# A decoder block: the order of SyncE's transfers within a quarter of the cross-attention loop, and the memory layout of its bias rows

## What is computed

```
# self-attention: one head, causal; only the row sums of exp(scores) are used
o = exp_qk.sum(-1);  y = relu(o @ fc1_w.T + fc1_b) @ fc2_w.T + fc2_b
x = layernorm(x + y)
# cross-attention: 16 heads of 32, keys = values = ctx, queries = x
logits  = einsum('bhqd,bhkd->bhqk', q, k) + bias
weights = softmax(logits / sqrt(32))
x = layernorm(x + (weights @ v) @ w_out)
# feed-forward with quantised weights (127 steps) and activations (32767 steps)
x = layernorm(x + q16(gelu(q16(x) @ q8(W_in) + b_in)) @ q8(W_out) + b_out)
```

## Time and profile before

| | before |
|---|---|
| three runs, us | 2289.72, 2265.87, 2286.9 |
| median, us | 2286.9 |
| profiled execution, us | 2284.26 |
| its span, us | 2282.5 |
| PE busy | 2111.4 us (93%) |
| DVE busy | 1735.8 us (76%) |
| ACT busy | 1082.4 us (47%) |
| POOL busy | 822.0 us (36%) |
| queue of SP's transfers, share of 16 DMA engines | 46.0% |
| queue of POOL's transfers, share | 22.9% |

### The profile page before, as it was taken

How to read it: one execution, slowest core, us unless ns; L and a number is a source line. 1 busy time by engine, 2 the same in 40 slices (tenths; PEclk the granted TensorE clock), 3 DMA queues, 4 the chain that set the end, 5 groups by cost and what they waited for, 6 DMA issues and landing times.

```text
span 2282.5 us, 32943 instructions
## 1 busy us (share of the span) xinstructions
PE 2111.4 (93%) x11904; PEld 1167.9 (51%) x11904; DVE 1735.8 (76%) x3296; ACT 1082.4 (47%) x1522; POOL 822.0 (36%) x802
## 2 busy tenths in 40 slices
PE   7999999984798998999999859999999699999997
PEld 3444444431586776777777524444444344444443
DVE  6768686865677897898898656777666488888885
ACT  1444444443444555555555224444444565555551
POOL 2122221222125555556455432222222134444442
PEclk9999999996779999999999779999999899999999
DMA  6334243457749969979975437888888656666662
GB/s 233 108 126 155 94 148 110 115 137 176 188 128 208 260 166 191 279 183 208 262 181 153 136 84 267 288 288 289 267 270 272 249 195 227 224 233 230 226 226 79
DMA packets 386626, 448.46 MB, mean 196 GB/s; under 512 B 279270, under 2 KB 279430, under 8 KB 368032
## 3 DMA queue, kind: packets, MB, share of 16 engines
q1 hardware_dynamic: 322448, 286.07, 46.0%
q0 software_dynamic: 64016, 160.28, 22.9%
HBM read 258.93 MB, written 138.73 MB: 174 GB/s over the span
## 4 chain that ended last, share of the span: by engine, by line
PE 82%; DVE 7%; issue 6%; ACT 1%; DMA 1%; POOL 1%; SPq 0%; DVEq 0%; POOLq 0%; ACTq 0%
PE ps_h L1708 19%; PE ps L1951 19%; PE ps_proj L600 10%; PE ps_o L1275 8%; PE ps_w L1304 7%; PE ps_s L620 5%; PE ps_m L1227 3%; PE ps_o L1271 3%; PE ps_m L1229 3%; PE ps_l L1253 3%; DVE rope_t L428 1%; PE ps_t L1289 1%; PE ps_l L1250 1%; DVE x_hi L411 1%; DVE stack L1099 1%
## 5 line engine op out<-in xcount | busy, mean ns | idle before, releaser
L1708 PE MATMUL ps_h<-xT,b_rows 128*128 128x512 f16 x2048 | 444.7, 381 | 13.1 <-DMA xT<-x_lo 13.1
L1951 PE MATMUL ps<-w,g_hi 128*128 128x512 f16 x1024 | 389.3, 380 | 21.1 <-DVE g_lo L1887 21.1
L1951 PE MATMUL ps<-w,g_lo 128*128 128x512 f16 x1024 | 389.1, 380 | 0.0
L1708 PEld LDWEIGHTS ps_h<-xT,b_rows 128*128 128x128 f16 x2048 | 200.9, 98 | 256.6 <-issue 16.6
L1549 ACT ACTIVATE h<-ps_h,b_rows 128x512 f32<-128x512 f32 x256 | 199.0, 777 | 241.5 <-PE ps_h L1708 241.5
L1275 PEld LDWEIGHTS ps_o<-vm,pT 128*128 128x128 f32 x2048 | 299.2, 202 | 13.0
L1099 DVE TENSOR_REDUCE stack<-ps_m 128x2 f16<-128x308 f32 x512 | 244.2, 479 | 55.3 <-PE ps_m L1229 53.6
L1275 PE MATMUL ps_o<-vm,pT 128*128 128x33 f32 x2048 | 284.8, 265 | 0.0
L1050 ACT ACTIVATE pT<-logit 128x512 f32<-128x512 f32 x320 | 199.0, 624 | 132.3 <-DVE logit L1117 131.4
L1622 DVE TENSOR_REDUCE amax_t<-h 128x1 f32<-128x2048 f32 x64 | 146.2, 2284 | 120.8 <-ACT h L1549 120.8
L1800 POOL TENSOR_TENSOR rstd<-vare,minus_half 128x1 f32<-128x1 f32 x64 | 152.3, 2380 | 208.5 <-DVE vare L1905 208.5
(11 more groups left out here) (182 smaller groups left out, 3840.1 us busy)
## 6 DMA issues: line engine op xcount, KB each, us to landing
hidden<-h POOLq DMA_DIRECT2D x64, 1024.0 KB, 6.7
hT<-hidden SPq DMA_DIRECT2D x64, 1024.0 KB, 6.2
xc<-x_cols SPq DMA_DIRECT2D x16, 1024.0 KB, 5.1
xr<-x_rows SPq DMA_DIRECT2D x16, 1024.0 KB, 5.5
x_rows<-x POOLq DMA_DIRECT2D x16, 1024.0 KB, 4.8
x1t<-x_rows SPq DMA_DIRECT2D x64, 256.0 KB, 3.8
bt_main<-bias_main SPq DMA_DIRECT2D x16, 1024.0 KB, 6.3
xres<-x_rows SPq DMA_DIRECT2D x64, 256.0 KB, 4.1
```

The source lines that it names most:

```text
L1708: mm = pe.matmul(ps_h[f % 4][:], w1[:, c, f * P:(f + 1) * P], xT[:, e, a, :, c, :], start=(a == 0 and c == 0), stop=(a == 1 and c == KC - 1))
L1951: mm = pe.matmul(ps[t][:], g[:, e, f, t * P:(t + 1) * P], w2[:, f, :], start=(f == 0 and a == 0), stop=(f == FC - 1 and a == 1))
```

## The change

Three things are changed. In SP's `quarter` the load of `x1t` comes first from q = 0 on, then the transpose of the stack, then that of the heads (up to q = -1: stack, heads, load). `kb` of batch 1 is loaded in SP's prologue, behind `ks` of batch 0, and not at q = -2. The bias rows lie in DRAM as [span, tile, partition, head, key], so that each partition's 16 x 154 float32 are one run of 9856 bytes, where before they were 16 runs of 616 bytes.

```diff
-                    pool.dma_start(b_rows[:, j], bias_rows[:, j * P:(j + 1) * P, :].rearrange("h p k -> p h k")).then_inc(
+                    pool.dma_start(b_rows[:, j], bias_rows[0, j]).then_inc(
                         rows_in[j], 16)
             load_ks(0, 0)
+            sp.wait_ge(done.kb_out, 16 * 2 * BLOCKS)
+            load_kb(1, 1)
 
             def quarter(s, b, i):
                 n = 4 * s + b
                 if 4 * n + i == -7:
                     sp.wait_ge(ident_ready, 2)
+                if n >= 0:
+                    load_x1(*span_at(s, b, i, 7))
+                turn_stack(*span_at(s, b, i, 4))
                 turn_heads(*span_at(s, b, i, 6))
-                turn_stack(*span_at(s, b, i, 4))
-                if 4 * n + i >= -5:
+                if -5 <= 4 * n + i < 0:
                     load_x1(*span_at(s, b, i, 7))
                 if 4 * n + i == -2:
                     load_v(0, 0)
                     load_bias(0, 1)
-                    load_kb(1, 1)
 
-                pool.dma_start(b_rows[:, t], bias_rows.rearrange("h (s t p) k -> t p h s k", t=4, p=P)[
-                    t, :, :, bass.ds(s, 1), :].rearrange("p h s k -> p h (s k)")).then_inc(rows_in[t], 16)
+                pool.dma_start(b_rows[:, t], bias_rows[s, t]).then_inc(rows_in[t], 16)
 
-        bias_rows=bias,
+        bias_rows=bias.reshape(HEADS, SEQ // BLK, 4, P, KEYS).transpose(1, 2, 3, 0, 4),
```

## The result

The changed kernel takes 2304.81 us (median of 13 runs, 2288.72 to 2316.81), the kernel before 2278.23 us beside it. The ratio is 1.0115 with a 95% interval of 1.0088 to 1.0142: slower, by about 27 us, where 2270 was forecast. The profiled execution took 2304.81 us.

The account below looks back on a forecast made before the run. PE was taken to bound the second-stage loop, losing time mostly in quarters with bias-row loads. Terms -6 (kb), -11 (bias rows) and +1 (order) gave -16 from 2284.3, 2268; with 2.6 for the median 2271, stated as 2270; range 2246 to 2300.

Parts of the forecast that it names:

- What bounds the kernel: Second-stage loop: PE limits; its 52 quarters have a floor of 539.2 us; better transfers can give back 31.4 us.
- kb, forecast -6: Ahead of the loop: early kb removes PE's 14.70 us wait; 6 us of gain remain, bounds 0 and 14.7.
- The landing near 563: Ahead of the loop: tile 4's heads' transpose lands at 563, so these maxima start about 8 us earlier.
- a second turn of the chain: Ahead of the loop: the next heads' transpose stands behind another stack's; half of the 8 us is gone.
- what was gained arrives there: At the wait for w_out, behind the first quarters: the time gained by early kb carries through; 6 us taken.
- Bias rows in one run, forecast -11: Loop quarters with bias-row loads: shorter landing disturbs others less; half of the 21.4 us lost there returns, 11 us.
- Crowding: Rival: in bias-row quarters transposes stand still while bias rows pass; layout gains only 3 us; 2279 us; chance 0.25.
- The order, forecast +1: SP's quarter: price nil in quiet quarters; in bias quarters xres lands after the work ahead, whatever the order; adds 1 us.
- quiet-quarter working: Quiet loop quarters: x1t at +2.4, stack +3.1, heads +4.8, xres +6.1, landing +10.1; 0.1 us of slack.
- d - 0.4: Loop quarters: a further delay d of xres costs about d less 0.4 us, paid every second quarter only.
- The late chain: Rival: heads' transpose behind the stack's issues slowly, making xres late in 20 loaded quarters; 41 us slower, 2312 us; chance 0.15.
- The clock: Rival: a shorter pause before 612 keeps PE's clock up in the slow 45 us; 14 us more, 2257; chance 0.20.

Follow-up runs that it names:

- e14: Against e7: POOL's load of bias rows issued in the middle of its quarter; ratio to the kernel before 0.9882.
- e1: Against the changed kernel: SP's quarter back in the old order (heads, stack, x1t, xres); ratio to the kernel before 1.0048.
- e3: Against the kernel before: only kb of batch 1 loaded early, in SP's prologue; old order and old bias-row layout; ratio 1.001.
- e7: Against the changed kernel: SP's quarter ordered xres, heads, stack, x1t; kb early, bias rows in one run; ratio to the kernel before 0.994.
- e8: Against e7: bias rows back in the old layout; ratio to the kernel before 0.9937.
- e9: Against the changed kernel: the two transposes swapped back, so x1t, heads, stack, xres; ratio to the kernel before 1.001.
- e12: Against e1: later bias-row loads bring one head of 16, the old order kept; ratio to the kernel before 0.9882.
- e15: Against e7: kb of batch 1 loaded where the kernel before loads it; ratio to the kernel before 0.9939.
- e2: Against the changed kernel: bias rows back in the old layout, new order and early kb kept; ratio to the kernel before 1.0146.
- e5: Against the changed kernel: each partition's bias rows read in four runs instead of one, 512 packets a load; ratio to the kernel before 1.0097.
- e11: Against the changed kernel: later bias-row loads bring one head of 16, the new order kept; ratio to the kernel before 0.9967.
- e6: Against the changed kernel: xres issued right behind x1t, ahead of both transposes (x1t, xres, stack, heads); ratio to the kernel before 1.0166.
- e10: Against the changed kernel: x1t put back behind both transposes, so stack, heads, x1t, xres; ratio to the kernel before 0.9991.

## Why the prediction was wrong

**What bounds the kernel** was read rightly: the losses lie in the quarters with bias rows, and most of the 31.4 us above the floor can be had: e14 takes 550.0 us for the 52 quarters, within 11 us of the 539.2 reckoned.

**kb, forecast -6.** The 14.70 us of wait went, as said, and came back in two pieces. SP and then PE in the changed kernel, to be laid beside the earlier trace rows:

```profile
555.10 5.43 SPq L840 DMA_TRANSPOSE qs<-stack  x1
560.63 1.21 SPq L827 DMA_TRANSPOSE q_heads<-q  x1
561.94 0.72 SPq L851 DMA_DIRECT2D x1t<-x_rows  x1
...
564.75 7.27 SPq L840 DMA_TRANSPOSE qs<-stack  x1
```

```profile
563.96 0.44 PE L1229 MATMUL ps_m<-kb,q_heads 128*128 128x308 f16 x1 [7.04 <-DMA q_heads<-q]
...
574.65 0.44 PE L1229 MATMUL ps_m<-kb,q_heads 128*128 128x308 f16 x1 [5.66 <-DMA q_heads<-q]
```

12.7 of the 14.7 us are waits for the heads now. The landing near 563 was forecast well; the first quarter, forecast at 572, came at 575.27, because the next stack took 7.27 us ahead of the next heads, a second turn of the chain that the working named and gave 4 us. With heads ahead of the stack and `kb` early (e1, e3, e7, e8, e9, e12 to e14) the two waits are 4.0 to 4.6 and 3.9 to 5.9 us, and the first quarter begins between 572.1 and 575.4. Even that does not reach the end: e15 against e7 shows no difference. DVE's wait for `w_out`, 9.87 us in the earlier trace rows, is 10.81 us in e7, ends 3 us earlier (605.48), and where quarter 7 then begins depends on how long the clock stays low behind it: 651.5 to 668.2 over the executions with `kb` early. The 5.4 us of the changed kernel at quarter 7 are of that kind: its `w_out` arrives at 609.50, later than before (608.38). What failed here is "what was gained arrives there": of the 6 us nothing that can be measured arrives (e3 1.001, e15 level with e7).

**Bias rows in one run, forecast -11.** The landing came as forecast (7.6 us for "6 to 8"), the gain did not. The mechanism that should have carried it, that loads with a shorter landing disturb the others less, is refuted: the same bytes hold up SP's transposes for about as long, in 2048 runs, in 512 or in 128 (5.6 us in e2, 6.5 in e5, 6.8 in the changed kernel, medians over the 12 loads in the new order). e7 and e8 are equal, and in the old order the layout in one run costs 12 us (e1 against e3) where the forecast had a gain of 11. The rival *Crowding* was nearest on this term (it gave it 3 us); what it lacked was the order's price.

**The order, forecast +1.** This is the step that broke the prediction. Its quiet-quarter working held: `x1t` at +2.3, the stack at +2.8, heads at +5.0, `xres` at +6.3, the residual on time at +10.2. (The stack right behind `x1t` takes 2.1 to 2.3 us to issue there and not 1.63, so the slack was smaller than reckoned.) The price was taken from there, and for the quarters with bias rows one sentence said that "xres lands when the work ahead of it is done, whatever the order; I add 1 us". That reckoned `xres` only, and put its delay at nothing. The heads, with 3 us of slack in a quiet quarter, were now behind a stack whose issue of 5.60 us stood in the earlier trace rows: 4.8 + (5.6 - 1.6) + 2.3 = +11.1 for a need at +10.37, from numbers already on the table. Measured, the issue became 6.5 to 8.7 us over the 12 loads, begun mostly 0.6 us behind POOL's load, and PE waited 19.8 us for the heads. e2 against e3 prices the step at 1.4%, e11 against e12 at 0.85%, after against e1 at 0.7%: 15 to 31 us, where 1 was forecast. The middle one stands without the bias rows' bytes, so the step failed beside other loads too, and not only beside the bias rows; how the price divides between late heads and late `xres` is not settled by the runs.

**The price of a wait.** The working charged a delay d as d - 0.4. In the 52 quarters PE's own waits rose by 10.3 us and its busy time by 16.4. In the kernels of the table the excess over 539.2 is 1.6 to 2.9 times the idle time, mostly about twice (before 31.4 and 16.0, after 58.1 and 26.3, e6 63.9 and 33.8, e7 19.1 and 9.7). On average a short wait here costs itself and again as much in clock; in e1 and e15, where single waits of 8 to 17 us make up most of the idle time, it is 1.6.

**The rivals.** *The late chain* (0.15, 2312 us) is nearest to the result: heads behind the stack, late in the 20 or so loaded quarters. It put the long issue on the heads themselves, which stay at 1.2 us; it is the stack's issue that grows. Its sign, "PE waits for `q_heads`", is what the trace shows. By its own rule its least value, 1.96 us of issue, would be 0.7 us late and cost 0.3 in 26 quarters, 7 us and not 13. *The clock* as a gain did not come here: from the first quarter to quarter 7 the granted clock is 0.66 (0.69 in the earlier trace rows); other executions have it, as e7's (0.74 from 570 to 660).

## What to carry to other kernels

When a transfer's place in an issuing queue is changed, check the loaded stretches with the longest issue seen there, for every transfer behind it and not only the last, against its own slack. Order the issuing queue by how soon each result is needed (here residual, heads, stack, token load: 0.994), and try another moment for a large load that starts with the queue's own work (0.9882 with both). Price a wait of the matrix engine with the clock behind it; here that about doubled it. And compare each variant with the one that differs from it in one thing only: e9 and e10 look level beside the kernel before, and faster beside e1.

## What was not expected of the hardware

- The issue of the large transpose from SP is a wait like any other: 1.6 us in a quiet quarter of the kernel before, 2.1 to 2.3 in the quietest quarters of the changed kernel, where it stands right behind the load of `x1t`, 2.4 to 3.4 there when it follows a load of 38.5 KB on POOL's queue (e11), 6.5 to 8.7 when it follows one of 616 KB (changed kernel). Everything behind it in SP's queue waits too.
- Sixteen times fewer runs shortened the load's landing from 11.8 to 7.6 us and never made the kernel faster by what can be measured; in the old order they made it 0.4% slower.
- A wait of 2.85 us of PE was followed by 8 us at half its clock.
- In one execution (e1) the DMA engines were busy for 24 us and moved 79 GB/s, and one load of bias rows took 24.2 us to land where the median of the 12 is 8.0.
- Open: why moving POOL's load to the middle of its quarter helps by 0.6% in all three orders, though in the old order it then lies across the transposes. The traces show shorter waits for `xres`, `q_heads` or both, but the load was tried at two places only, in e14 the stack beside a load still takes 5.4 us to issue at the median, and the executions of one kernel differ by up to 31 us (e15).
